# Post-norm layer on one core: all 16 shared feed-forward blocks before the experts, none in the last stage

## The reference, cut to what matters

```python
normed = x * rsqrt(mean(x * x) + 1e-08) * norm_weight
shared = maximum(normed @ sw1 + sb1, 0) @ sw2 + sb2          # 256 -> 1024 -> 256, every row
scores, idx = top_k(sigmoid(normed @ router_w.T), 2)
w = scores / (sum(scores) + 1e-06)
h = maximum(einsum('td,edh->teh', normed, ew1) + eb1, 0)
eo = einsum('teh,eho->teo', h, ew2) + eb2                     # 256 -> 1024 -> 256, two experts a row
out = layernorm(x + shared + sum_over_chosen(w * eo))
```

## Time and profile before

| What | us |
|---|---|
| median of three executions | 1530.94 |
| their range | 1525.81 to 1532.79 |
| span of the profiled execution | 1646.1 |
| PE, DVE, ACT, POOL busy in it | 1399.0, 1197.8, 983.0, 545.8 |
| stage of blocks 0 to 9 and the scatter, in it | 699.9 to 900.2 |
| last stage, in it | 1512.9 to 1646.1 |

### The profile page before, as it was taken

One profiled execution on the slowest core, in us unless ns is written; L12 is line 12 of the kernel. 1 busy time (PEld: TensorE's weight loads), 2 busy tenths in 40 slices (PEclk: granted clock), 3 DMA queues, 4 the chain that ended last, 5 costly groups with the idle time before them and its releaser, 6 DMA issues. The chain is left out here.

```text
span 1646.1 us, 31319 instructions
## 1 busy us (share of the span) xinstructions
PE 1399.0 (85%) x9849; PEld 1050.4 (64%) x9920; DVE 1197.8 (73%) x2480; ACT 983.0 (60%) x2014; POOL 545.8 (33%) x532
## 2 busy tenths in 40 slices
PE   4899999999999986991198999999999999997486
PEld 2444444444444435891198888888888888886475
DVE  3888878878888855860065888888888888885467
ACT  4688878878888875850044545545545545543355
POOL 5222222212221003547500433433433433443542
PEclk7999999999999997995599899999999999998697
DMA  7000000000000214113200655555555555550332
GB/s 307 1 2 27 2 28 9 20 28 2 27 2 14 65 39 154 39 51 129 83 0 26 207 164 197 176 168 192 176 175 186 177 179 180 181 164 31 94 106 90
DMA packets 106408, 160.42 MB, mean 97 GB/s; under 512 B 12928, under 2 KB 85888, under 8 KB 105152
## 3 DMA queue, kind: packets, MB, share of 16 engines
q1 hardware_dynamic: 97040, 132.10, 24.6%
q0 software_dynamic: 9264, 27.01, 4.9%
HBM read 121.86 MB, written 37.22 MB: 97 GB/s over the span
## 5 line engine op out<-in xcount | busy, mean ns | idle before, releaser
L470 DVE TENSOR_REDUCE att_mx<-att_psA 128x1 f32<-128x512 f32 x512 | 339.1, 683 | 57.9 <-PE att_psA L269 55.6
L387 ACT ACTIVATE att_prob<-att_psB 128x512 f32<-128x512 f32 x512 | 290.1, 603 | 79.9 <-PE att_psB L279 67.5
L1431 ACT ACTIVATE exp_h<-exp_psU,ew_b 128x256 f32<-128x256 f32 x312 | 146.8, 470 | 277.6 <-PE exp_psU L1389 210.6
L1401 PE MATMUL exp_psD<-exp_w2h,exp_hh 128*128 128x256 f32 x624 | 215.3, 345 | 50.1 <-DVE exp_hl L1466 43.5
L1462 DVE CAST exp_hh<-exp_h 128x256 fp32r<-128x256 f32 x312 | 209.1, 670 | 38.2 <-ACT exp_h L1431 33.2
L269 PE MATMUL att_psA<-att_qk 96*128 96x512 bf16 x512 | 195.8, 384 | 8.3 <-DVE att_mx L470 4.8
L1401 PEld LDWEIGHTS exp_psD<-exp_w2h,exp_hh 128*128 128x128 f32 x624 | 132.7, 213 | 90.1 <-DVE exp_hl L1466 89.3
L1402 PE MATMUL exp_psD<-exp_w2l,exp_hh 128*128 128x256 f32 x624 | 190.0, 304 | 0.0
L1403 PE MATMUL exp_psD<-exp_w2h,exp_hl 128*128 128x256 f32 x624 | 189.6, 304 | 0.0
L1466 DVE TENSOR_TENSOR exp_hl<-exp_h,exp_hh 128x256 fp32r<-128x256 f32 x312 | 173.5, 556 | 10.8
L1387 PE MATMUL exp_psU<-exp_xh,exp_w1h 128*128 128x256 f32 x624 | 177.8, 285 | 2.1 <-DVE exp_w1l L1457 2.1
(11 more groups left out here) (187 smaller groups left out, 3338.0 us busy)
## 6 DMA issues: line engine op xcount, KB each, us to landing
ew_w<-ew SPq DMA_DIRECT2D x40, 1024.0 KB
exp_w<-ew SPq DMA_DIRECT2D x38, 1024.0 KB, 6.0
exp_xs<-slots_x SPq DMA_DIRECT2D x39, 256.0 KB, 3.9
slots_y<-exp_ys POOLq DMA_DIRECT2D x39, 256.0 KB, 4.3
slots_x<-pre_acc SPq DMA_DIRECT2D x9, 1024.0 KB, 14.9
ew_b<-eb SPq DMA_DIRECT2D x39, 128.0 KB, 3.5
att_xt<-xT SPq DMA_DIRECT2D x8, 512.0 KB, 4.6
attn_rows<-att_ob SPq DMA_DIRECT2D x8, 512.0 KB, 3.2
```

What stands on the lines that cost most here:

```text
L387: act.activation(prob[:, n % PR, :], psB[n % 2][:, :], ACT.Exp, scale=SCALE).then_inc(s_exp, 1)
L470: dve.reduce_max(mx[:, g % 2, n % U:n % U + 1], psA[A_BANK[n % U]][:, :], AX_X).then_inc(s_max, 1)
L1401: pe.matmul(ps, hh[:, h, rows], w2h[:, h, :], start=(h == 0), stop=False)
```

## The change

Every block is done in `shared_and_dispatch`: its `NB` is 16, so its loop makes six passes (blocks 2 to 13), with blocks 14 and 15 after it. The shared bias is added once for each block, to the block's own two tiles, and those of blocks 0 and 1 stand ahead of `place`. `combine` has no `Shared`, no work on PE, no ReLU on ACT and no hidden parts on DVE; its gathers, sums, norm and stores are as they were.

```diff
-    NB = m.early_blocks
+    NB = TILES // 2
...
-            def add_bias(n, j):
-
-                n.wait(dve, shared.added, 1, -1 if j == 0 else 0)
-                some = m.acc[:, bass.ds(n.n * 4 + (2 * j - 8), 2), :]
+            def add_bias(n):
+
+                some = m.acc[:, bass.ds(n.n * 2, 2), :]
                 dve.tensor_tensor(some, some, m.sb2[:, :].unsqueeze(1).to_broadcast([P, 2, m.sb2.shape[1]]), ALU.add).then_inc(s_bias, 1)
...
-                add_bias(n, 0)
-                n.wait(dve, s_bias, 2, -3)
+                add_bias(n)
+                n.wait(dve, s_bias, 1, 0)
                 shared.add(dve, n.before())
-                add_bias(n, 1)
-
-            assert 2 * (NB - 2) == TILES // 2
+
             shared.rows_lo(dve, Nth(0))
             choose()
             shared.rows_lo(dve, Nth(1))
             shared.rows_lo(dve, Nth(2))
+            add_bias(Nth(0))
+            add_bias(Nth(1))
+            dve.wait_ge(s_bias, 1)
             shared.add(dve, Nth(0))
             place()
...
-            dve.wait_ge(s_bias, 2 * (NB - 2))
+            dve.wait_ge(s_bias, NB)
             shared.add(dve, Nth(NB - 1))
...
-    NB = TILES // 2 - m.early_blocks
...
-        shared = Shared(a, m, 2 * m.early_blocks, buffers=2)
...
-            shared.rows_lo(dve, Nth(0))
             for slot in range(TILES + 2):
...
-                    if i >= shared.first:
-                        Nth((i - shared.first) // 2).wait(dve, shared.added, 1, 1)
...
-                n, h = divmod(2 * (slot - 1), shared.HC)
-                if 0 <= n < NB:
-                    shared.hidden_lo(dve, Nth(n), h)
-                    shared.hidden_lo(dve, Nth(n), h + 1)
-                if h == 2 and 0 <= n and n + 1 < NB:
-                    shared.rows_lo(dve, Nth(n + 1))
-                if h == 0 and 2 <= n <= NB + 1:
-                    shared.add(dve, Nth(n - 2))
-
-        @block.tensor
-        def _(pe):
-
-            for n in range(NB + 1):
-                for part in range(4):
-                    if n < NB:
-                        shared.up(pe, Nth(n), 2 * part, 2 * part + 2)
-                    if n >= 1:
-                        shared.down(pe, Nth(n - 1), part, 4)
...
-            shared.rows_hi(act, Nth(0))
...
-                n, h = divmod(2 * slot, shared.HC)
-                if n < NB:
-                    shared.relu(act, Nth(n), h)
-                    shared.relu(act, Nth(n), h + 1)
-                if h == 2 and n + 1 < NB:
-                    shared.rows_hi(act, Nth(n + 1))
```

More of the change, by code:

```diff
@@ L578, in _ @@
             groups(dve, period, after_loop)
-EARLY_BLOCKS = 10
 class NormInputs:
@@ L1621, in __init__ @@
         lists = (2 * T + E * (list_tile - 1)) // list_tile
-        self.early_blocks = EARLY_BLOCKS
         self.acc = acc
```

## The result

| | median us | range |
|---|---|---|
| before | 1530.44 | 1525.81 to 1532.79 |
| after | 1595.64 | 1594.03 to 1599.03 |

The change makes the kernel 65.2 us slower: 1.0427 of the time before, with a 95% interval of 1.0402 to 1.0452. The prediction said 1598 us, +67.

The account below looks back on a forecast made before the run. The prediction took PE to bound the shared blocks' stage, and POOL's gathers the last stage after the change. For the timed executions +68.6 + 1.4 - 3.1 = +66.9 on 1530.9 gave 1598 us, range 1568 to 1606.

Parts of the forecast that it names:

- Six blocks at 0.119 us a matmul: Stage of the shared blocks: 576 more matmuls on PE at 0.119 us each, with nothing covering them, +68.6 us.
- The scatter's margin: End of the shared blocks' stage: scatter through at 815, 8 us before PE's end, so it covers nothing.
- Bias additions: Two moved ahead of `place` delay slots, scatter, first weights and block 2's hidden parts: +1.4 us, bounds 0 and 1.4.
- The last stage: Combine stage: bound by POOL's gathers, 1.26 us each, once the shared work leaves; gives back 3.1 us.
- The holds: Engine stalls beside POOL's scatters (75.7 us) and gathers (40.7 us), taken to exist in the profiled execution alone.
- The first rival: The holds are real and in the timed executions too: 1557 us, up to 1577 if in part; chance 0.17.
- The gap between span and time: Whole kernel: profiled span 115.2 us above the timed median, put down to the holds, against the skill's 6.2 us.
- The long scatter: Shared blocks' stage: scatter outlasts PE and hides the six blocks, needing 2.5 us or more each; 1508 to 1528 us; chance 0.05.

Follow-up runs that it names:

- b_again: The kernel before, profiled once more with no edit: 1530.36 us, ratio 1.0001, profiled span 1530.2 us.
- no_six: The changed kernel with blocks 10 to 15 computed nowhere, their tiles getting the bias alone: 1529.25 us, ratio 0.9998 to the kernel before.
- early12: The changed kernel with only twelve blocks early and four left in the last stage: 1549.49 us, ratio 1.013 to the kernel before.
- bias_late: The changed kernel with the bias additions of blocks 0 and 1 behind `place`, not ahead: 1591.87 us, ratio 1.0414 to the kernel before.

## Why the prediction was right, and where it was not

**The size, by its terms.** The two comparable profiles are `b_again` (1530.2) and after (1592.3), 62.1 us apart.

| term | forecast | measured | from |
|---|---|---|---|
| six blocks on PE | +68.6 | +68.4 | first matmul to last `add`, against `no_six` |
| bias additions ahead of `place` | +1.4 | +0.5 | the same, `no_six` against before |
| scatter sets the stage's end before | 0 | -2.0 | last `add` to the barrier: 2.96, now 0.98 |
| last stage | -3.1 | -1.8 | 92.8, now 91.0 |
| stages that the change doesn't touch | 0 | -3.1 | -1.3, -1.5 and -0.3, between single executions |
| sum | +66.9 | +62.0 | spans: +62.1 |

The medians differ by 65.2. The profiled execution after lies 1.6 us below its median and that of `b_again` 1.5 above, which are the 3 us in untouched stages, so I count these as spread between executions and no part of the change. The other terms make +65.1. Each is read from single executions and is uncertain by about 1 us, so a sum as close as this is in part luck.

**Six blocks at 0.119 us a matmul: right.** Nothing covers them but 2 us, since PE ran without a gap before and does so after. `early12` gives the price a second time. From the first shared matmul at 701.76 to the last `add` it takes 143.48 us, so its two blocks cost 143.48 - 119.87 = 23.6 and the four others 188.26 - 143.48 = 44.8, or 11.8 and 11.2 us a block against a forecast of 11.4.

**The scatter's margin: wrong by some 10 us.** "The scatter is through at 815, 8 us earlier" was read from a trace in which DVE and PE stood still during the scatter. Three things were off. With both at work each scatter takes 1.328 us instead of 1.274, (817.58 - 733.93) / 63 against (812.00 - 731.75) / 63, and the last is through 3.4 us later on that account. The chain of PE and DVE ended some 3 us sooner than worked out by taking a hold of 75.7 us off the held trace: from the first shared matmul to the last `add` the two profiles of the kernel before differ by (899.30 - 701.38) - 119.33 = 78.6 us. And the prediction took the scatter to be done when its bytes stop. They stop within 3 us of the last issue in both traces, but in `b_again` POOL passes the barrier only 5.8 us later. The step that failed is a margin of 8 us put together from a held trace and from the last byte. It was worth 2 us only because PE and the scatter happen to end together, and that is luck.

**Bias additions: an overestimate within the bounds.** PE does wait for block 2's hidden parts, for 1.0 us, but up to the last `add` 0.5 us are left of it, which is within the spread of single executions. `bias_late` didn't separate the two, as its additions still stood ahead of the same parts.

**The last stage: right in kind, less in size.** It changed from DVE with POOL close behind to POOL alone, for 92.8 us against a forecast of 92.5, and 91.0 against 89.4. In the kernel before the two bounds are nearly equal already, as its waits show:

```profile
POOL out_g L1529 <- issue: 17.4, 57, 0.3
...
DVE out_y L1551 <- DMA out_g<-slots_y,all_slot: 5.0, 3, 4.0
...
POOL out_g L1529 <- DVE out_y L1552: 1.8, 6, 0.3
```

POOL waited for DVE only 6 times, and no longer than the 0.3 us that lie between any two gathers. The page's chain of `b_again` gives most of this stage to PE, which is busy without a gap from 1451 to 1508. But DVE is busy for 9.3 to 9.6 of every 10 us from 1455 to 1515, and the one wait through which the chain passes to ACT and PE is 0.16 us. So PE and DVE are even there. The prediction had only said that PE fits beside DVE. With the change the gathers come every 1.289 us instead of 1.26, 62 x 0.03 = 1.8 us more. `no_six` and `early12` show the same 90 us from the first gather: once two of the six blocks have left, no more comes back.

**The holds: the conclusion right, the reason wrong.** The prediction needed to know whether the 1530.94 contained them, and said no, because their sum of 116.4 closes with the excess of 115.2. The sum was good: `b_again`, which has neither hold, is 1646.1 - 1530.2 = 115.9 us shorter. That it closed to 1.2 us was in part luck: the first hold of PE was 78.6 us and not 75.7, and the stage grew by only 76.0, because the scatter's end covers 2 us of it. But "the holds exist in the profiled execution alone" says more than that sum does, which is only that the timed executions have none. That they come with the chip and not with the profiler was not among the cases. The price was the profile's forecast, 1672 us for a span of 1592.3.

The first rival, real holds with a time of 1557, has its own answer. On a chip that has them, the change costs 46.5 us and not 26.2. The stage of the shared blocks grows by 343.5 - 277.15 = 66.4 us there too, memset to memset. The last stage gives back 25.7 and not 43.8, since a hold that came from gathers doesn't leave with PE's work: the 64 gathers stay, and DVE stands beside them.

**The gap between span and time.** The Trainium skill (Runtime: NRT & Kernel Launch, section "The ~15µs preamble/postamble breakdown") gives a constant gap of about 6.2 us, with the profile the longer. The prediction held the trace's 115.2 against it, and that was no counterexample, since span and time were of two executions. Where both are of one execution, the span here is the shorter, by 1.65 to 1.87 us in all but 7 of 116 executions and by up to 4.25 in those. So the gap is nearly constant here, and this case shows neither the 6.2 us nor the sign. The span here runs from the first instruction to the last, and no run shows whether that is the quantity meant there.

**The long scatter: not decided in its own terms.** On a chip with the hold it can't cover anything, and the pair with the doubled scatter stays 44 us apart. At 1.33 us a scatter, far from the 2.5 that it needed, it played a part of 2 us only.

## What to carry to other kernels

Moving work out of a stage gives back only down to that stage's next bound. Here the gathers stood 1.8 us below, so the first two blocks that left took everything there was, and each block after them cost its full 11.4 us on PE. Before reading a stall from a profile, hold its span against a time of the same execution, or against a second profile of the same kernel: two of one kernel were 116 us apart here, and every long wait in the one was absent from the other. A duration read beside idle engines can't be carried over to busy ones without a margin: a scatter took 4% longer beside busy ones here. Nor does it always go that way, since the gathers came every 1.271 us in `b_again` beside a busy PE and every 1.289 with the change and PE idle. And the last byte of a transfer is not yet the moment at which the engine that waits for it goes on; here 5.8 us lay between the two, barrier included.

## What the runs showed of the hardware

- **A chip can hold its compute engines while POOL issues indirect DMAs back to back.** On one chip the stage of the shared blocks was longer by 35.5, 76.0 and 160.6 us than without a hold, with 32, 64 and 128 scatters that took 40.7, 81.2 and 167.0 us to issue. PE, DVE and ACT were nearly idle meanwhile (13.93, 2.73 and 3.84 of 83.40 us). On another chip the kernel with 64 scatters had none of it. The kernel before takes 1642 us on the one and 1530 on the other, 7% apart, with ratios of the change of 1.0273 and 1.0427. The cause is open.
- **An indirect DMA of 128 rows costs POOL about 1.3 us, whichever way it goes.** The scatter runs at 1.274 us beside held engines and at 1.328 on the chip without a hold, beside busy ones; the two differ in the chip as well. The gather runs at 1.271 us in `b_again` and 1.289 after the change, and at 1.38 on the chip with the hold.
- **A profile adds almost nothing here.** The span of a profiled execution is 1.7 to 1.8 us below its own time in the three shown (1592.3 and 1594.03, 1530.2 and 1531.87, 1688.6 and 1690.39), and those times lie within 0.3% of the medians of their kernels.
